# The block quantizer of the 2,048-column tiles: one routine exchanged for the other in a macaron transformer layer

## What is computed

```
x = x + 0.5 * ffn(layernorm(x))
x = x + attention(layernorm(x))
x = x + 0.5 * ffn(layernorm(x))
```

```
def _mx_dequant(t):
    blocks = t.reshape(rows, feat // 32, 32)
    max_abs = jnp.max(jnp.abs(blocks), axis=-1)
    scales = jnp.maximum(max_abs / 448, 1e-30)
    q = (blocks / scales[..., None]).astype(jnp.float8_e4m3fn).astype(jnp.float32)
    return (q * scales[..., None]).reshape(rows, feat)
def _mx_linear(x2d, w):
    return _mx_dequant(x2d) @ _mx_dequant(w).T
gate = _mx_linear(x2d, gate_w); up = _mx_linear(x2d, up_w)     # (8192, 2048) each
out = _mx_linear(silu(gate) * up, down_w)                      # (2048, 8192)
```

## Time and profile before

| what | value |
|---|---|
| median of 3 runs | 33140.6 us (33128.33 to 33162.52) |
| time of the profiled execution | 33130.49 us |
| its span on the slowest core (core 3) | 33129.0 us |
| spans of the 8 cores | 33104.5 to 33129.0 us |
| mean granted TensorE clock | 0.61 on every core |
| VectorE busy | 14774.0 us, 45%, 20320 instructions |
| TensorE matmul busy | 6012.2 us, 18% |
| ScalarE busy | 3882.5 us, 12% |
| mean busy share of the DMA engines, by their largest queue | 11.0% |

### The profile page before, as it was taken

The page is one execution under the profiler, slowest core; times in us unless marked ns, Lnnn a source line. Parts: engine busy times, 40 slices in busy tenths (PEclk is TensorE's granted clock), DMA queues, the critical chain, the costliest instruction groups (busy, mean ns, idle before and its releaser), DMA issues.

```text
span 33129.0 us, 103336 instructions; the slowest of 8 cores (33104.5 to 33129.0 us)
## 1 busy us (share of the span) xinstructions
PE 6012.2 (18%) x21664; PEld 2363.4 (7%) x21664; DVE 14774.0 (45%) x20320; ACT 3882.5 (12%) x3928; POOL 0.2 (0%) x4
## 2 busy tenths in 40 slices
PE   0011111111111111111110320231232212222225
PEld 0000000000000000000000110110010100000012
DVE  6555455544555545555455235321322254454540
ACT  1111111111111111111111001000101111111110
POOL 0000000000000000000000000000000000000000
PEclk9855555555555555555555665665665656666667
DMA  0000000000000000000001221123111100000013
GB/s 26 27 24 18 14 22 24 24 18 14 23 24 24 16 14 24 24 24 12 18 24 28 77 72 55 63 94 108 33 41 40 34 28 22 22 17 22 17 41 116
DMA packets 1151383, 1132.02 MB, mean 34 GB/s; under 512 B 963488, under 2 KB 1047584, under 8 KB 1094304
## 3 DMA queue, kind: packets, MB, share of 16 engines
q1 hardware_dynamic: 1150752, 1125.41, 11.0%
HBM read 727.82 MB, written 214.96 MB: 28 GB/s over the span
## 4 chain that ended last, share of the span: by engine, by line
DVE 44%; DMA 19%; PE 18%; ACT 10%; issue 5%; ACTq 2%; DVEq 2%; SPq 0%
DVE SC L261 5%; PE PB L352 4%; DVE SC L238 3%; PE PB L388 3%; DVE SC L258 3%; PE PB L357 3%; DMA SCB<-SCB 2%; DVE mblk L154 2%; DMA BIGC<-dqhT 2%; ACTq L761 2%; PE PB L700 2%; DVE SC L235 2%; DMA BIGC<-SCB 2%; DVEq L761 2%; PE PB L457 2%
## 5 line engine op out<-in xcount | busy, mean ns | idle before, releaser
L352 PE MATMUL PB<-BIGC,BIGA 128*128 128x512 bf16 x4096 | 1485.9, 543 | 15251.1 <-DMA dqhT<-SCB 8012.6
L364 DVE TENSOR_TENSOR SC<-SC,PB 128x512 f32<-128x512 f32 x256 | 176.1, 688 | 4230.1 <-ACT SC L361 4230.1
L388 PE MATMUL PB<-BIGA,BIGC 128*128 128x512 bf16 x4096 | 1019.0, 415 | 3617.2 <-DMA BIGC<-dqhT 3617.2
L352 PEld LDWEIGHTS PB<-BIGC,BIGA 128*128 128x128 bf16 x4096 | 517.9, 131 | 16218.6 <-issue 16118.7
L261 DVE SCALAR_TENSOR_TENSOR SC<-SC 128x512 f32<-128x512 f32 x2304 | 1594.4, 692 | 172.2
L154 DVE TENSOR_REDUCE mblk<-SC 128x16 f32<-128x512 f32 (+1 forms) x600 | 757.1, 1262 | 1988.8 <-DMA SC<-up_w 718.0
L700 PE MATMUL PB<-BIGC,BIGA 128*128 128x512 bf16 x2048 | 657.8, 492 | 4473.1 <-DVE SCB L272 3250.7
L175 ACT ACTIVATE SC<-SC,cst 128x2048 f32<-128x2048 f32 x216 | 432.3, 2001 | 8065.5 <-DVE SC L172 8065.2
L361 ACT ACT_TABLE_LOAD x256 | 328.4, 1283 | 6758.9 <-PE PB L357 6758.9
L238 DVE SCALAR_TENSOR_TENSOR SC<-SC 128x512 f32<-128x512 f32 x1536 | 1062.7, 692 | 115.3
L258 DVE TENSOR_SCALAR SC<-SC 128x512 f32<-128x512 f32 x2304 | 984.0, 427 | 184.9 <-issue 10.3
(11 more groups left out here) (119 smaller groups left out, 13410.3 us busy)
## 6 DMA issues: line engine op xcount, KB each, us to landing
BIGC<-dqhT SPq DMA_DIRECT2D x96, 2048.0 KB, 7.7
SC<-gate_w SPq DMA_DIRECT2D x64, 1024.0 KB, 4.9
SC<-up_w SPq DMA_DIRECT2D x64, 1024.0 KB, 4.9
SC<-down_w SPq DMA_DIRECT2D x64, 1024.0 KB, 4.7
dqhT<-SCB SPq DMA_DIRECT2D x384, 128.0 KB, 1.7
dqwTg<-BIGC SPq DMA_DIRECT2D x16, 2048.0 KB, 6.3
dqwTu<-BIGC SPq DMA_DIRECT2D x16, 2048.0 KB, 6.3
SCB<-wk SPq DMA_DIRECT2D x64, 512.0 KB, 4.2
```

Source lines behind the costliest of these rows:

```text
L352: P.t(lambda e, kb=kb, tt=tt: e.matmul(PB[0][:], lhsT=BIGA3[:, kb, tt * 128:(tt + 1) * 128], rhs=BIGCg[:, kb, :], start=(kb == 0), stop=(k ...
L388: P.t(lambda e, kb=kb: e.matmul(PB[2][:], lhsT=BIGC64[:, kb, :], rhs=BIGAq[:, kb, :], start=(kb == 0), stop=(kb == NKI - 1)), inc=('t', 1) ...
```

## The change

The four calls of `quant_cheap` become calls of `quant_ladder` with the same arguments. The calls on 128x512 tiles, which were `quant_ladder` before, and all the rest of the kernel stay as they are; no line number moves.

```
@@ -331,7 +331,7 @@
         for tt in range(NT):
             P.dma(SC2[:], x_in[tt * 128:(tt + 1) * 128, :], waits=P.wv())
             layernorm_sc2()
-            quant_cheap(SC2[:], D, SCB1[:])
+            quant_ladder(SC2[:], D, SCB1[:])
             P.dmat(BIGA3[:, :, tt * 128:(tt + 1) * 128], SCB1[:], waits=P.wv())
```

## The result

The changed kernel takes 40,813.7 us (median of 8 runs, 40,780.1 to 40,895.6) against 33,174.65 us before (8 runs, 33,128.3 to 33,220.9). The ratio is 1.2307, with a 95% interval of 1.2293 to 1.2320, so the change costs 7,607 to 7,697 us. The forecast was 7,654 us more and 40,790 us in all, in a range of 40,720 to 40,890. The profiled execution took 40,795.14 us; the sum had been made against the profiled execution before and gave 40,784.

The account below looks back on a forecast made before the run. Bound by a serial chain with nearly no overlap: profiled 33,130.49 us plus 7,654 us (216 calls at 35.434 us) gives 40,784, or 40,795 from the runs' median; forecast 40,790 us, range 40,720 to 40,890, chance 0.91.

Parts of the forecast that it names:

- The reading that nothing overlaps: Whole kernel: one engine works at a time, so every us added inside the routine moves the kernel's end by one us.
- The same 19 instructions: Added per call on 128x2048: nine pairs of comparison and scalar_tensor_tensor plus one tensor_tensor, 35.434 us with gaps.
- The count and the prices: 216 calls, added instructions at durations from the earlier trace plus gaps of 0.076 to 0.079 us: 7,654 us.
- the 460 us of the rival: Copies L233 and L256 on 128x2048 run at the two-tensor rate, 2,292 ns: 460 us more, 41,250 us; chance 0.03.
- The waits for ScalarE: In each call VectorE waits for the second of two Exp activations, 4.27 us on 128x2048, unchanged by the exchange.
- The reading that a flush comes on top of each duration: Drain as long as its operation adds 7,336 us, 48,130 in all (some 47,030 by the skill's page); chance 0.01.
- The term of stalls: VectorE stalls of 0.37 us, one a call: 80 us more, kept in the range; chance 0.04 of over 40,900 us.
- the 28 us that were kept for TensorE's clock: Longer rests shift TensorE's speed-up in 21 loops behind quantizing stages, 1.33 us each: 28 us either way, in the range.
- the added work hides: The 35.4 us a tile runs during transfers, in VectorE's 9.79 us idle ahead of L154: 33,140 us; chance 0.01.
- the other side: Whole-kernel result not slower: within 0.2 per cent (66 us) had chance 0.01, faster 0.005; slower had 0.985.

Follow-up runs that it names:

- the share of 128 calls: The ladder only on the 128 tiles of gate and up weights, other 88 calls as in the kernel before: 37,781.5 us, ratio 1.1373.
- the cover: Kernel before, own routine, with two load and two output buffers so weight tiles' loads and transposes run under neighbour tiles' quantizing: 31,615.4 us, 0.951.
- the last version: Kernel before with a third routine (bitwise and, large constant, no Ln or Exp) on all 600 calls, plus two load and two output buffers: 19,173.1 us, 0.577.

## Why the prediction was right

*What bounds the kernel.* The reading that nothing overlaps held. The same 19 instructions cost 7,639 us on the kernel before and 7,626 us on the one with hidden transfers, and the share of 128 calls was that of their number.

*The count and the prices.* A call costs 35.37 us in the timeline, 35.43 in the sum. The durations from the earlier trace rows came back unchanged in all groups, and the gap is 0.075 to 0.081 us. By stage the waits grew by 5,089, 2,278 and 282 us where 5,103, 2,268 and 283 were forecast.

*The copies.* 1,227 ns as costed, so the 460 us of the rival did not come. The rule of the Trainium skill (page "VectorE: DVE Perf Modes", perf-mode tier table), that fp32 copies and tensor_scalar share a tier, agrees with this row.

*The waits for ScalarE.* 4.27 us a call before and after, as argued.

*The drain.* The reading that a flush comes on top of each duration (the Trainium skill, section "The DRAIN you can't avoid" of the same page) is excluded as a cost: the gap behind 2,292 ns is that behind 692 ns, and the tile in the timeline grew by 35.37 us. The prediction also took the whole gap for the drain's cost, which its rows could not show; a second drain takes 0.049 us, and the sum holds whatever the gap is made of. The term of stalls stayed under the 80 us that were kept for it: VectorE's stalls went from 144 and 61 us to 179 and 76 us, counted as for the run with two drains.

*What else moves.* The 11 us between the sum (40,784) and the profiled execution (40,795) stand beside 10.5 us more of TensorE busy time (6,022.7 against 6,012.2) and 7.1 us more on ScalarE, inside the 28 us that were kept for TensorE's clock. Which of them it is, no run here separates. The prediction read TensorE's lower clock out of durations. The granted clock bears this out for the second row tile (0.50 from 1362.7 to 1364.0 us, 1.00 from 1366.0 on), but it reads 1.00 all through the first tile, whose 16 matmuls took 0.408 us each. So the 28 us rest on durations and not on that record.

*The rivals.* That the added work hides is refuted in the stronger form too: with buffers made for it, the transfers hid and the ladder did not. No run shows a mechanism that would have put the result on the other side.

*What was luck.* The total came within 24 us of the forecast, closer than the kernel before repeats itself: its median was 33,140.6 us in the three runs that the forecast had and 33,174.65 in eight. The level that it started from, 40,790 - 7,654 = 33,136, was 39 us too low and the added cost 15 us too high, and the two made up for each other in part. What the forecast can be credited with is the 7,654 us against 7,639, in an interval of 7,607 to 7,697.

Two forecasts of the experiments were off, both too hopeful: the cover (1,753 forecast, 1,593 came) and the last version (14,117 against 14,038). For the cover the trace gives two parts on the slowest core, transfers sized 49 us too high and 199 us more of TensorE busy time, and leaves some 30 us open. No experiment tried them one by one.

## What to carry to other kernels

When the chain's shares by engine are near the busy shares and one queue waits as often as the routine is called, price a change by counting instructions: duration by form, plus the gap, times the calls. Here the forecast of the added 7.6 ms came out within what the runs can tell, 0.6 per cent either way. The largest gain in these runs came from fewer operations for the same rounding (a power of two from the bits, a rounding by a constant), because each one is paid in full; a second buffer hid the transfers, but not the engine's own chain. Take durations for the same operation and shape, and where one is missing, compare it with its neighbours at another shape.

## What the runs showed of the hardware

A second drain of VectorE behind an instruction costs 0.049 us, whether the operation took 0.69 or 2.29 us. A bitwise and on int32 views of 128x2048 runs in 1,227 ns, as fast as an fp32 comparison.

Stalls of some 0.4 to 0.5 us, in which VectorE waits for nothing that the profile shows, were more in the kernels with more code: 144 for 20,320 instructions, 179 for 24,424, and 286 for 20,320 with two drains each. What they are was not shown.

TensorE's time for the same 64 matmuls differed between cores of one execution. In the kernel with hidden transfers and the routine from before, core 7 and core 2 show (timeline, TensorE only):

```profile
17504.60 19.18 PE L407 MATMUL PB<-BIGA,BIGC 128*128 128x512 bf16 x64 [11.47 <-DMA BIGC<-dqhT]
```

```profile
17453.36 15.95 PE L407 MATMUL PB<-BIGA,BIGC 128*128 128x512 bf16 x64 [11.40 <-DMA BIGC<-dqhT]
```

That is 0.300 against 0.249 us a matmul, after the same rest. Both start at the lower of the two levels, 1.2 GHz (granted clock 0.50 from 17,504 to 17,510 us on core 7 and from 17,453 to 17,457 on core 2). The second part of the burst makes the difference. A stretch of it on core 7, then on core 2 (the number before the DMA share is the granted clock):

```profile
17511.00:17523.00 12.00, 12.00 (x47) 5.00 (x46) 0.00 (x0) 0.00 (x0) 0.00 (x0) 0.81 0.00 0
```

```profile
17458.00:17469.00 11.00, 11.00 (x53) 4.92 (x51) 0.00 (x0) 0.00 (x0) 0.00 (x0) 1.00 0.00 0
```

Core 2 rises to the upper level, 2.4 GHz, and core 7 only to 0.81 of it, where a matmul takes 0.26 us in place of 0.21. What holds core 7 down was not looked for. In this stage all four cores of its die (4 to 7) have such bursts of 19 us, and cores 0 to 3 took 1,018 to 1,023 us for the group, so none to speak of; core 7, with the most time in this group but for core 6, ended 0.2 ms after core 2.
